# First mixture of experts: token numbers in the rows, results scattered to token order by GpSimd, combination by plain loads, tile loop written out

## The chip, the cores and the metric

The kernel runs on one core of a Trainium2 chip. The metric is the device time of one execution in microseconds (us), given as the median of the executions of a kernel. One execution more is recorded by the hardware profiler; its page and its trace are what is read here. Engines are called PE (TensorE, with PEld for its weight loads), DVE (VectorE), ACT (ScalarE), POOL (GpSimd) and SP (SyncE, which issues DMAs); "SPq", "ACTq" are the queues of their sequencers.

## The reference

Two decoder layers over 4 x 1024 tokens of 256 numbers, fp32: cross attention, then self attention with a mixture of experts, cross attention again, and a second mixture of experts in which each expert chooses its tokens. The change lies in the first mixture:

```python
x = _ln(src + attn, n1_g, n1_b)
xr = x.reshape(-1, d)
logits = xr @ moe_gate_w + moe_gate_b
top_v, top_i = jax.lax.top_k(logits, 2)
wts = jax.nn.softmax(top_v, axis=-1)
chosen = jnp.max(top_i, axis=-1)

def expert(W1, B1, G, Bt, W2, B2, rsc):
    hh = xr @ W1 + B1
    hh = jax.nn.gelu(_ln(hh, G, Bt), approximate=False)
    return (hh @ W2 + B2) * rsc + xr
outs = jax.vmap(expert)(w1, b1, ln_g, ln_b, w2, b2, res_scale)
sel = jnp.take_along_axis(outs.transpose(1, 0, 2), chosen[:, None, None], axis=1)[:, 0]
moe = sel * jnp.sum(wts, axis=-1, keepdims=True)
return _ln(x + moe.reshape(b, s, d), n2_g, n2_b)
```

Each of the 4096 tokens goes through one of eight experts (256 to 512 to 256).

## The kernel before

`self_attention_moe` runs stages one after the other, each a block in which the five engines follow their own instruction lists and meet at semaphores. A block ends when all engines are done, and the next starts after it.

`attention_out` makes the rows `src_sb` (128 partitions x 32 tiles x 256) in eight chunks of four tiles. Beside this, SP fills the DRAM buffer `gathered_in` (4992 rows) with zeros from one tile (L1234), and waits for it at the end of the block. The rows must be zero where no token lands.

`route_tokens` computes for each token its slot in a list sorted by expert, each expert's share rounded up to tiles of 128 rows; there are MT = 39 tiles. GpSimd then scatters `src_sb` to `gathered_in` with one indirect DMA for each of the 32 tiles (L1449), while SP loads the experts' weights, 8 MB.

`expert_tiles` works off the 39 tiles. Each engine runs a body for each tile k, with four buffers (U = 4) and a lead of three tiles (AHEAD = 3). The order in each body is written out by hand:

- SP loads the rows of tile k+3 (L1557), once the bias sum of tile k-1 and the transposes of tile k have freed their buffers.
- PE transposes the rows of tile k+3 (L1580), transposes the normalized hidden rows of tile k (L1601), multiplies tile k-1 by the second weights (L1613) and tile k+3 by the first (L1590).
- ACT stores the result of tile k-2 to `gathered_out` (L1646), copies the transposed rows of tile k+3 (L1630), applies the gelu to tile k (L1640).
- DVE finishes tile k-1 (L1682, into the buffer `xb` that holds rows plus bias), normalizes the hidden rows of tile k+2 (L1675), adds the bias of tile k+3 and takes its moments (L1666 to L1671).
- POOL adds the second bias to the rows of tile k+1 (L1719), which writes `xb` and so waits until the store of tile k-3 has landed (`y_stored`), and then makes the reciprocal deviation of tile k+3 (L1710, L1712), for which it waits for the moments.

The number of the expert is read from SBUF into a register of each engine that uses it. The bodies of tiles 4 to 35 stand in a hardware loop of eight rounds; the first four and the last three are written out.

`combine_experts` goes back to token order in eight chunks of four tiles. POOL gathers the results with 32 indirect DMAs (L1761) by the slots, two chunks ahead, and makes the reciprocal deviation of each chunk (L1769, L1773). DVE multiplies the gathered rows by the token's weight and adds `src_sb` (L1795), takes the moments (L1800, L1803), makes the shift (L1820), then the moments of the next chunk, then for its own chunk the product with the gain (L1809) and the sum into `x_sb` (L1811). ACT normalizes (L1784). There are two buffers `z` and one set of the small vectors.

## Time and profile before

| | |
|---|---|
| median of 3 executions | 2141.88 us (2141.66 to 2144.35) |
| profiled execution, its own time | 2131.64 us |
| its span, first to last instruction | 2130.0 us |
| mean granted clock of TensorE | 0.896 of 2.4 GHz |
| busy: PE, DVE, ACT, POOL | 1744.8, 1278.8, 936.2, 450.0 us |
| routing and scatter | 1266.5 to 1319.5 us |
| expert tile loop | 1319.5 to 1494 us |
| combination | 1495.2 to 1561.7 us |

The windows view gives the busy time of each engine in a stretch, with the number of instructions, then the granted clock of TensorE (PEclk), the busy share of the 16 DMA engines and GB/s. The timeline view gives one row for a run of like instructions: start, duration (of a run, from its first start to its last end), engine, line, operation, tile written<-tiles read, count, and in brackets how long the engine had been idle before and what released it ("issue": nothing that the profile shows). The view of a source line gives durations in ns as least/median/most, and for DMAs the time from the start of their issue to landing. Start times count from the span's start.

### The profile page before, as it was taken

Reading aid. Unit: us, or ns where it says so; the run is one execution under the profiler, and the core shown is the slowest. Engines: PE = TensorE matmul, PEld = TensorE weight load, DVE = VectorE, ACT = ScalarE, POOL = GpSimd, SP = SyncE. Lnnn points to the kernel's source line nnn. Section 1 sums busy time; section 2 is a strip of 40 time slices with the busy share of each in tenths; the row PEclk is TensorE's granted clock in tenths of the full one; section 3 lists DMA queues with packets and bytes.
Section 4 is the critical chain, followed back from the end, with each engine's and each line's share of the span. In section 5 each row is a group of like instructions: output and inputs, shape, how many; then the busy total and the mean of one; then the engine's idle time right before and its main releaser. Section 6 shows DMA issues by size and latency. Waiting matters only on the chain. (4 is left out here: it accounts for less than half of the span.)

```text
span 2130.0 us, 30316 instructions
## 1 busy us (share of the span) xinstructions
PE 1744.8 (82%) x10569; PEld 837.0 (39%) x10570; DVE 1278.8 (60%) x2189; ACT 936.2 (44%) x1708; POOL 450.0 (21%) x467
## 2 busy tenths in 40 slices
PE   5899698399999999999997851999057996259997
PEld 3466454022222222222223640677034663146654
DVE  5344344788999998999951450666684554470221
ACT  3423166077777777777774210444243332102110
POOL 4200044710000000000001435333752001020443
PEclk8899899599999999999999975999579998657999
DMA  4000068712111221112104016121200003310452
GB/s 133 1 1 2 16 210 297 157 23 50 36 37 36 54 54 36 37 36 53 20 1 172 1 49 235 55 64 57 76 10 1 2 2 120 130 31 11 102 135 30
DMA packets 114592, 137.07 MB, mean 64 GB/s; under 512 B 16672, under 2 KB 90656, under 8 KB 114208
## 3 DMA queue, kind: packets, MB, share of 16 engines
q1 hardware_dynamic: 99632, 113.47, 19.3%
q0 software_dynamic: 9216, 16.79, 3.4%
q10 hardware_dynamic: 5616, 5.11, 0.7%
q8 instruction: 80, 1.31, 0.3%
q14 instruction: 48, 0.39, 0.1%
HBM read 78.31 MB, written 56.89 MB: 63 GB/s over the span
## 5 line engine op out<-in xcount | busy, mean ns | idle before, releaser
L984 DVE TENSOR_REDUCE sa_mhalf<-sa_a 128x2 f32<-128x1024 f32 x512 | 602.4, 1221 | 63.9 <-PE sa_a L1093 60.9
L1071 ACT ACTIVATE sa_e<-sa_b 128x512 f32<-128x512 f32 x1024 | 532.0, 602 | 207.2 <-PE sa_b L1120 203.0
L1120 PE MATMUL sa_b<-sa_q,sa_k 112*128 112x512 bf16 x1024 | 310.7, 385 | 3.8 <-ACT sa_e L1071 3.8
L1130 PE MATMUL sa_ops<-sa_e,sa_v 128*17 128x512 f32 x2048 | 270.3, 599 | 6.6 <-ACT sa_e L1071 1.3
L1093 PE MATMUL sa_a<-sa_k,sa_q 48*128 48x512 bf16 x1024 | 176.7, 398 | 44.2 <-DMA sa_k<-k_parts 24.9
L1120 PEld LDWEIGHTS sa_b<-sa_q,sa_k 112*128 112x128 bf16 x1024 | 83.9, 97 | 278.9 <-ACT sa_e L1071 231.6
L1245 POOL TENSOR_TENSOR ao_var<-ao_mv,x_eps_pow 128x4 f32<-128x4 f32 x8 | 1.6, 202 | 762.0 <-DVE ao_mv L1314 762.0
L213 DVE TENSOR_REDUCE xa_mx<-xa_rows 128x16 f32<-128x1024 f32 x64 | 78.3, 1224 | 98.6 <-PE xa_rows L445 98.6
L1093 PEld LDWEIGHTS sa_a<-sa_k,sa_q 48*128 48x128 bf16 x1024 | 43.9, 93 | 193.6 <-DVE sa_mhalf L984 78.8
L360 ACT ACTIVATE xa_pT<-xa_cols 128x1024 f32<-128x1024 f32 x64 | 62.1, 1022 | 84.9 <-PE xa_cols L477 84.9
L2475 DVE TENSOR_TENSOR sw_hT<-sw_p,sw_act 128x512 f32<-128x512 f32 x32 | 22.1, 692 | 102.0 <-PE sw_p L2420 102.0
L1590 PE MATMUL ex_hps<-ew_w,ex_xT 128*128 x156 | 77.3, 619 | 1.9 <-ACT ex_xT L1630 1.9
L445 PE MATMUL xa_rows<-xa_kblk,xa_qT 64*128 64x256 f32 x512 | 73.1, 407 | 6.1 <-DVE xa_mx L213 5.3
L544 PE MATMUL xa_cols<-c_ctxT,c_wts 128*128 128x256 f32 x16 | 7.4, 646 | 85.7 <-PEq L43 72.2
L1613 PE MATMUL ex_yps<-ew_w,ex_hT 128*128 x312 | 73.9, 380 | 1.8 <-ACT ex_hT L1640 1.8
L2388 POOL DMA_INDIRECT out_x<-sw_yo,tc_idx x32 | 49.9, 1558 | 105.7 <-DVE sw_yo L2482 98.7
L2464 ACT ACTIVATE sw_act<-sw_p 128x512 f32<-128x512 f32 x32 | 19.1, 597 | 118.9 <-PE sw_p L2414 118.9
L1630 ACT ACTIVATE ex_xT<-ex_xps 128x256 f32<-128x256 f32 x39 | 15.0, 384 | 126.0 <-PE ex_xps L1580 126.0
L1640 ACT ACTIVATE ex_hT<-ex_tps,sm_bt,sm_g 128x128 f32<-128x128 f32 x156 | 58.8, 457 | 20.9 <-PE ex_tps L1601 17.3
L2414 PE MATMUL sw_p<-sw_xT,tc_w 128*128 128x512 f32 x128 | 62.0, 608 | 1.2 <-ACT sw_xT L2453 1.2
L514 PE MATMUL xa_front<-c_wts,xa_oS 128*128 128x256 f32 x256 | 59.5, 386 | 2.6 <-DVE xa_oS L228 2.6
L1130 PEld LDWEIGHTS sa_ops<-sa_e,sa_v 128*17 128x17 f32 x2048 | 34.9, 95 | 67.2 <-ACT sa_e L1071 54.1
(326 smaller groups left out, 2735.3 us busy)
## 6 DMA issues: line engine op xcount, KB each, us to landing
k_parts<-sp_kpart SPq DMA_DIRECT2D x96, 128.0 KB, 1.8
sa_q<-q_parts SPq DMA_DIRECT2D x64, 192.0 KB, 5.2
sa_k<-k_parts SPq DMA_DIRECT2D x64, 192.0 KB, 5.6
tc_w<-in_L_ffn_W SPq DMA_DIRECT2D x24, 512.0 KB, 6.5
q_parts<-sp_qpart SPq DMA_DIRECT2D x16, 384.0 KB, 3.1
expert_in<-ao_zero SPq DMA_DIRECT2D x1, 4992.0 KB, 23.1
expert_out<-ex_xb ACTq DMA_DIRECT2D x39, 128.0 KB, 1.7
v_groups<-sp_vt SPq DMA_DIRECT2D x8, 544.0 KB, 4.0
```

Of the source, the lines that this page charges most:

```text
L213: nc.vector.tensor_reduce(mx[:, t], rows[:].rearrange("p r (n k) -> p (r n) k", k=SC), axis=X, op=ALU.max).then_inc(max_done, 1)
L360: nc.scalar.activation(pT[:, 4 * half + 2 * part:4 * half + 2 * part + 2], cols[:, 2 * part:2 * part + 2], ACT.Exp, scale=SCALE).then_inc( ...
L445: last = nc.tensor.matmul(rows[:, r, half * D:(half + 1) * D], qT[part, half, tokens], kblk[part, c // 2, half, CT * r:CT * (r + 1)], star ...
L514: last = nc.tensor.matmul(front[:, bank, (t % 2) * D:(t % 2 + 1) * D], oS[:, k, t * P:(t + 1) * P], wts[:, 3, k], start=(k == 0), stop=(k ...
L984: nc.vector.tensor_reduce(mhalf[par][:, half, head:head + PAIRED + 1:PAIRED, t], aps[at][:], axis=X, op=ALU.max).then_inc(a_used, 1)
L1071: nc.scalar.activation(ex[kt % 2][:, head], bps[(2 * (2 * s + qc) + i) % 3][:], ACT.Exp, scale=SCALE).then_inc(exp_done, 1)
L1093: last = nc.tensor.matmul(aps[at][:, h // PAIRED], qs[s][rows, h, q0:q0 + P], ks[s][rows, h, half * CW:(half + 1) * CW], start=True, stop= ...
L1120: nc.tensor.matmul(bps[(2 * (2 * s + qc) + i) % 3][:], ks[s][:, head, kt * P:(kt + 1) * P], qs[s][:, head, qc * CW:(qc + 1) * CW], start=T ...
L1130: last = nc.tensor.matmul(ops[32 * head:32 * head + VW], vs[s][:, kt, head], ex[kt % 2][:, head], start=(kt == 0), stop=(kt == KT - 1))
L1590: last = nc.tensor.matmul(hps[j % 2][:], xT[j % 2][:, half], ew["w1"][:, half, ds(e, 1), :], start=(half == 0), stop=(half == HALVES - 1))
L1613: last = nc.tensor.matmul(yps[j % 2][:, 0:D], hT[j % 2][:, f], ew["w2"][:, f, ds(e, 1), :], start=(f == 0), stop=(f == FK - 1))
L2414: last = nc.tensor.matmul(p1[f % 2][:], w1[e % 3][:, half, f * P:(f + 1) * P], xT[e % 2][:, half], start=(half == 0), stop=(half == HALVES ...
```

## The change

The rows of `src_sb`, `gathered_in` and the loaded tiles become 264 numbers long. The eight columns behind the 256 hold the token's number as an integer; rows in which no token lands hold numbers past the last token, from 4096 on, each another one. These are written to DRAM by a second DMA behind the zeros. In the tile loop POOL copies the column of token numbers to a small tile of its own, adds the bias, makes the deviation, and issues the store of tile k-2 itself, as an indirect DMA that scatters the 128 result rows to `moe_out` by token number. ACT stores nothing. Four buffers for the loaded rows are allocated; two of them were spent tiles before. The hardware loop becomes 39 bodies in a row. The combination loads the results with eight plain DMAs on SP's queue, has four buffers `z` and two sets of the small vectors; the product with the gain moves from DVE to POOL, and DVE's last sum for a chunk stands behind the moments of the chunk three later.

```diff
+ROW = D + 8
...
-        zero = sb("zero", [P, D])
+        zero, spare = sb("zero", [P, D]), sb("spare", [P, MT, ROW - D], i32)
...
+                rows = gathered_in.rearrange("(k p) d -> p k d", p=P)
                 sp.wait_ge(zero_made, 1)
-                sp.dma_start(gathered_in.rearrange("(k p) d -> p k d", p=P),
-                             bc(zero[:], 1, [P, MT, D])).then_inc(cleared, 16)
-                sp.wait_ge(cleared, 16)
+                sp.dma_start(rows[:, :, 0:D], bc(zero[:], 1, [P, MT, D])).then_inc(cleared, 16)
+                sp.wait_ge(spare_made, 1)
+                sp.dma_start(rows[:, :, D:ROW], spare[:].bitcast(fp32)).then_inc(cleared, 16)
+                sp.wait_ge(cleared, 32)
...
+                nc.gpsimd.iota(spare[:], [[P, MT], [0, ROW - D]], base=TOKENS, channel_multiplier=1).then_inc(spare_made, 1)
...
+                nc.gpsimd.iota(src_rows[:, :, D:ROW].bitcast(i32), [[P, TILES], [0, ROW - D]], base=0, channel_multiplier=1
+                               ).then_inc(iota_made, 1)
+                pool.wait_ge(iota_made, 3)
                 pool.wait_ge(slots_ready, 1)
                 for t in range(TILES):
                     pool.indirect_dma_start(out=gathered_in, out_offset=bass.IndirectOffsetOnAxis(ap=slot_i[:, t:t + 1], axis=0),
-                                            in_=src_sb[:, t, :], in_offset=None).then_inc(scattered, 16)
+                                            in_=src_rows[:, t, :], in_offset=None).then_inc(scattered, 16)
...
-        xg = [b[:].rearrange("p t e -> p (t e)") for b in spent] + [sb(f"xg{i}", [P, D]) for i in range(len(spent), U)]
+        xg = [sb(f"xg{i}", [P, ROW]) for i in range(U)]
+        token = [sb(f"token{i}", [P, 1], i32) for i in range(U)]
...
-            for j in range(U):
-                body(j, 0, j, True)
-            with eng.Fori(1, MT // U) as i:
-                for j in range(U):
-                    body(i * U + j, i, j, True)
-            for k in range(MT // U * U, MT):
-                body(k, k // U, k % U, False)
+            for k in range(MT):
+                body(k, k // U, k % U, k + AHEAD < MT)
...
-                def store(k, j):
-                    act.wait_ge(y_ready, k + 3)
-                    act.dma_start(gathered_out[ds(P * k, P), :], xb[j][:]).then_inc(y_stored[j], 16)
-
                 def body(k, turn, j, ahead):
-                    if later(k, 2):
-                        store(k - 2, (j - 2) % U)
...
                 def add_b2(k, turn, j):
                     e = expert(pool, k)
                     pool.wait_ge(x_loaded[j], 16 * (turn + 1))
-                    if later(k, U):
+                    if k >= U:
                         pool.wait_ge(y_stored[j], 16 * turn)
-                    nc.gpsimd.tensor_tensor(xb[j][:], xg[j][:], ew["b2"][:, ds(e, 1), :].rearrange("p o f -> p (o f)"),
+                    nc.gpsimd.tensor_copy(token[j][:], xg[j][:, D:D + 1].bitcast(i32)).then_inc(token_kept, 1)
+                    pool.wait_ge(token_kept, k + 1)
+                    nc.gpsimd.tensor_tensor(xb[j][:], xg[j][:, 0:D], ew["b2"][:, ds(e, 1), :].rearrange("p o f -> p (o f)"),
                                             ALU.add).then_inc(xb_ready, 1)
 
                 def body(k, turn, j, ahead):
-                    if not isinstance(k, int) or k + 1 < MT:
+                    if k + 1 < MT:
                         add_b2(k + 1, turn + (j + 1) // U, (j + 1) % U)
                     if ahead:
                         make_rstd(k + AHEAD, (j + AHEAD) % U)
+                    if k >= 2:
+                        scatter(k - 2, (j - 2) % U)
+
+                def scatter(k, j):
+
+                    pool.wait_ge(y_ready, k + 3)
+                    pool.indirect_dma_start(out=moe_out, out_offset=bass.IndirectOffsetOnAxis(ap=token[j][:, 0:1], axis=0),
+                                            in_=xb[j][:], in_offset=None).then_inc(y_stored[j], 16)
 
                 pool.wait_ge(ew["b2_scaled"], 1)
                 pool.wait_ge(y_ready, 2)
                 for k in range(AHEAD):
                     make_rstd(k, k)
                 turns(pool, body)
-
-
-def combine_experts(nc, x_sb, src_sb, eps_pow, w, wsum, slot_i, gathered_out):
-
+                for k in range(MT - 2, MT):
+                    scatter(k, k % U)
...
-                sp.dma_start(n2g[:], w["n2_g"].partition_broadcast(P)).then_inc(loaded, 16)
+                for c in range(CHUNKS):
+                    sp.dma_start(yg[:, CT * c:CT * (c + 1)], moe_out[CW * c:CW * (c + 1)].rearrange("(t p) d -> p t d", p=P)
+                                 ).then_inc(y_loaded[c], 16)
+                    if c == 1:
+                        sp.dma_start(n2g[:], w["n2_g"].partition_broadcast(P)).then_inc(loaded, 16)
...
-                def gather(c):
-                    for t in range(CT * c, CT * (c + 1)):
-                        pool.indirect_dma_start(out=yg[:, t, :], out_offset=None, in_=gathered_out,
-                                                in_offset=bass.IndirectOffsetOnAxis(ap=slot_i[:, t:t + 1], axis=0)
-                                                ).then_inc(gathered[c], 16)
-
-                gather(0)
-                gather(1)
+                def invert(c):
+                    par = c % 2
+                    pool.wait_ge(ln_stats, CT * (c + 1))
+                    nc.gpsimd.tensor_tensor(var[par][:], mv[par][:, :, 1], eps_pow[:, 0], ALU.add).then_inc(var_done, 1)
+                    pool.wait_ge(var_done, c + 1)
+                    if c >= 2:
+                        pool.wait_ge(zn_ready, CT * (c - 1))
+                    nc.gpsimd.tensor_tensor(rstd[par][:], var[par][:], eps_pow[:, 1], ALU.pow).then_inc(rstd_ready, 1)
+
+                def scale(c):
+                    zs = z[c % BUFFERS]
+                    pool.wait_ge(zn_ready, CT * (c + 1))
+                    nc.gpsimd.tensor_tensor(zs[:], zs[:], bc(n2g[:], 1, [P, CT, D]), ALU.mult).then_inc(zg_ready, 1)
+
+                invert(0)
+                pool.wait_ge(loaded, 16)
                 for c in range(CHUNKS):
-                    pool.wait_ge(ln_stats, CT * (c + 1))
-                    nc.gpsimd.tensor_tensor(var[:], mv[:, :, 1], eps_pow[:, 0], ALU.add).then_inc(var_done, 1)
-                    pool.wait_ge(var_done, c + 1)
-                    if c >= 1:
-                        pool.wait_ge(zn_ready, CT * c)
-                    nc.gpsimd.tensor_tensor(rstd[:], var[:], eps_pow[:, 1], ALU.pow).then_inc(rstd_ready, 1)
-                    if c + 2 < CHUNKS:
-                        gather(c + 2)
+                    if c + 1 < CHUNKS:
+                        invert(c + 1)
+                    scale(c)
...
-                    dve.wait_ge(gathered[c], 16 * CT)
-                    if c >= 2:
-                        dve.wait_ge(x_done, c - 1)
+                    dve.wait_ge(y_loaded[c], 16)
...
+                def make_shift(c):
+                    par = c % 2
                     dve.wait_ge(rstd_ready, c + 1)
                     dve.wait_ge(ln_stats, CT * (c + 1))
+                    if c >= 2:
+                        dve.wait_ge(zn_ready, CT * (c - 1))
+                    nc.vector.scalar_tensor_tensor(out=shift[par][:], in0=mv[par][:, :, 0], scalar=-1.0, in1=rstd[par][:],
+                                                   op0=ALU.mult, op1=ALU.mult).then_inc(shift_ready, 1)
+                    dve.wait_ge(shift_ready, c + 1)
+
+                def finish(c):
+
+                    xs = x_sb[:, CT * c:CT * (c + 1), :]
+                    dve.wait_ge(zg_ready, c + 1)
+                    nc.vector.tensor_tensor(xs, xs, z[c % BUFFERS][:], ALU.add).then_inc(x_done, 1)
+                    dve.wait_ge(x_done, c + 1)
+
+                moments(0)
+                moments(1)
+                for c in range(CHUNKS):
+                    make_shift(c)
+                    if c + 2 < CHUNKS:
+                        moments(c + 2)
                     if c >= 1:
-                        dve.wait_ge(zn_ready, CT * c)
-                    nc.vector.scalar_tensor_tensor(out=shift[:], in0=mv[:, :, 0], scalar=-1.0, in1=rstd[:], op0=ALU.mult,
-                                                   op1=ALU.mult).then_inc(shift_ready, 1)
-                    if c + 1 < CHUNKS:
-                        dve.wait_ge(shift_ready, c + 1)
-                        moments(c + 1)
-                    finish(c)
+                        finish(c - 1)
+                finish(CHUNKS - 1)
...
-    gathered_in = nc.dram_tensor("expert_in", (MT * P, D), fp32, kind="Internal").ap()
-    gathered_out = nc.dram_tensor("expert_out", (MT * P, D), fp32, kind="Internal").ap()
+    gathered_in = nc.dram_tensor("expert_in", (MT * P, ROW), fp32, kind="Internal").ap()
+    moe_out = nc.dram_tensor("moe_out", (TOKENS + MT * P, D), fp32, kind="Internal").ap()
```

## Rows read from the trace of the kernel before

**Rows 1.** Windows: the tile loop, and a later stretch with TensorE partly idle.

```profile
1340.00:1475.00 135.00, 135.00 (x594) 94.94 (x593) 93.74 (x166) 61.33 (x163) 50.28 (x99) 1.00 0.21 65
...
1600.00:1620.00 20.00, 13.62 (x48) 6.74 (x48) 10.02 (x6) 6.43 (x9) 10.81 (x5) 1.00 0.00 0
```

**Rows 2.** Timeline of PE in the tile loop.

```profile
1469.81 1.89 PE L1613 MATMUL ex_yps<-ew_w,ex_hT 128*128 x8
...
1473.91 1.89 PE L1613 MATMUL ex_yps<-ew_w,ex_hT 128*128 x8
```

**Rows 3.** Timeline of POOL in the tile loop.

```profile
1389.46 0.19 POOL L1710 TENSOR_TENSOR ex_var<-ex_mv,x_eps_pow 128x1 f32<-128x1 f32 x1 [2.03 <-DVE ex_mv L1671]
1389.73 0.55 POOL L1712 TENSOR_TENSOR ex_rstd<-ex_var,x_eps_pow 128x1 f32<-128x1 f32 x1
1390.55 0.73 POOL L1719 TENSOR_TENSOR ex_xb<-ex_xg,sm_b 128x256 f32<-128x256 f32 x1 [0.27 <-issue]
```

**Rows 4.** Line L1449, the routing's scatters: the last six, then all 32.

```profile
L1449 POOL DMA_INDIRECT expert_in<-sm_src,sm_slot_i x6: 956/960/960, 1307.3 to 1313.7; - x6
...
DMA to landing us min/median/max: 2.4/2.4/2.4
...
DMA to landing us min/median/max: 2.4/5.5/6.6
```

**Rows 5.** Landing of the gathers (L1761), and of the last stage's accumulating scatters (DMA view).

```profile
DMA to landing us min/median/max: 2.7/2.8/3.4
...
out_x<-sw_yo,tc_idx POOLq DMA_INDIRECT x32, 3.9
```

**Rows 6.** Timeline of all engines in a middle chunk of the combination.

```profile
1522.14 1.02 POOL L1761 DMA_INDIRECT co_yg<-expert_out,sm_slot_i  x1 [0.19 <-issue]
...
1522.18 1.67 DVE L1795 SCALAR_TENSOR_TENSOR co_z<-co_yg,sm_wsum,sm_src 128x256 f32<-128x256 f32 x4
...
1525.36 1.20 DVE L1809 TENSOR_TENSOR co_z<-co_z,co_n2g 128x1024 f32<-128x1024 f32 x1
...
1529.22 1.67 DVE L1795 SCALAR_TENSOR_TENSOR co_z<-co_yg,sm_wsum,sm_src 128x256 f32<-128x256 f32 x4
```

**Rows 7.** The same timeline: a power by itself, then the last chunk.

```profile
1520.91 1.03 POOL L1773 TENSOR_TENSOR co_rstd<-co_var,x_eps_pow 128x4 f32<-128x4 f32 x1
...
1554.80 1.22 DVE L1811 TENSOR_TENSOR x_x<-x_x,co_z 128x1024 f32<-128x1024 f32 x1
1554.90 1.99 POOL L1773 TENSOR_TENSOR co_rstd<-co_var,x_eps_pow 128x4 f32<-128x4 f32 x1
...
1557.13 2.07 ACT L1784 ACTIVATE co_z<-co_z,co_shift,co_rstd 128x256 f32<-128x256 f32 x4 [4.71 <-DVE co_shift L1820]
...
1560.49 1.22 DVE L1811 TENSOR_TENSOR x_x<-x_x,co_z 128x1024 f32<-128x1024 f32 x1
```

**Rows 8.** The same timeline: the combination's start.

```profile
1495.24 0.34 SPq L1755 DMA_DIRECT2D co_n2g<-in_L_ffn_n_g  x1
...
1502.74 1.67 DVE L1795 SCALAR_TENSOR_TENSOR co_z<-co_yg,sm_wsum,sm_src 128x256 f32<-128x256 f32 x4 [10.80 <-DMA co_yg<-expert_out,sm_slot_i]
```

**Rows 9.** A plain load of 512 KB (DMA view), and a POOL product of 128x1024 (line L1252).

```profile
x_x<-in_x SPq DMA_DIRECT2D x1, 512.0 KB, 3.9
...
L1252 POOL TENSOR_TENSOR ao_xr<-ao_xr,ao_n1g x8: 2337/2342/2349, 1165.2 to 1253.2; 128x1024 f32<-128x1024 f32 x8
```

**Rows 10.** Timeline of the tile loop's end, and ACT's stores in the DMA view.

```profile
1483.88 0.55 POOL L1712 TENSOR_TENSOR ex_rstd<-ex_var,x_eps_pow 128x1 f32<-128x1 f32 x1
...
1490.23 2.09 ACTq L1646 DMA_DIRECT2D expert_out<-ex_xb  x2
...
expert_out<-ex_xb ACTq DMA_DIRECT2D x39, 128.0 KB, 1.7
```

**Rows 11.** DMA view: the zeros. Timeline: the routing's first scatter.

```profile
expert_in<-ao_zero SPq DMA_DIRECT2D x1, 4992.0 KB, 23.1
...
1274.18 1.24 POOL L1449 DMA_INDIRECT expert_in<-sm_src,sm_slot_i  x1 [7.25 <-DVE sm_slot_i L1501]
```

More of the change, by code:

```diff
@@ L1658, in _ @@
                 turns(act, body)
-                for k in range(MT - 2, MT):
-                    store(k, k % U)
             @block.vector
@@ L1734, in _, with combine_experts @@
                 turns(pool, body)
-def combine_experts(nc, x_sb, src_sb, eps_pow, w, wsum, slot_i, gathered_out):
+                for k in range(MT - 2, MT):
+                    scatter(k, k % U)
+def combine_experts(nc, x_sb, src_sb, eps_pow, w, wsum, moe_out):
+    BUFFERS = 4
     with ExitStack() as ctx:
@@ L1743, in combine_experts @@
         yg = sb("yg", [P, TILES, D])
-        z = [sb(f"z{i}", [P, CT, D]) for i in range(2)]
-        stats, mv = sb("stats", [P, CT, 6]), sb("mv", [P, CT, 2])
-        var, rstd, shift = sb("var", [P, CT]), sb("rstd", [P, CT]), sb("shift", [P, CT])
+        z = [sb(f"z{i}", [P, CT, D]) for i in range(BUFFERS)]
+        stats, mv = ([sb(f"{n}{i}", [P, CT, k]) for i in range(2)] for n, k in (("stats", 6), ("mv", 2)))
+        var, rstd, shift = ([sb(f"{n}{i}", [P, CT]) for i in range(2)] for n in ("var", "rstd", "shift"))
         loaded, z_ready, stats_done, ln_stats = sem("loaded"), sem("z_ready"), sem("stats_done"), sem("ln_stats")
-        gathered = [sem(f"gathered{c}") for c in range(CHUNKS)]
-        var_done, rstd_ready, zn_ready, zg_ready, x_done = (sem("var_done"), sem("rstd_ready"), sem("zn_ready"),
-                                                                      sem("zg_ready"), sem("x_done"))
-        shift_ready = sem("shift_ready")
+        y_loaded = [sem(f"y_loaded{c}") for c in range(CHUNKS)]
+        var_done, rstd_ready, shift_ready = sem("var_done"), sem("rstd_ready"), sem("shift_ready")
+        zn_ready, zg_ready, x_done = sem("zn_ready"), sem("zg_ready"), sem("x_done")
         with nc.Block() as block:
@@ L1779, in _ @@
                 for c in range(CHUNKS):
+                    zs, par = z[c % BUFFERS], c % 2
                     act.wait_ge(shift_ready, c + 1)
@@ L1783, in _ @@
                     for t in range(CT):
-                        nc.scalar.activation(z[c % 2][:, t], z[c % 2][:, t], ACT.Identity, bias=shift[:, t:t + 1],
-                                             scale=rstd[:, t:t + 1]).then_inc(zn_ready, 1)
+                        nc.scalar.activation(zs[:, t], zs[:, t], ACT.Identity, bias=shift[par][:, t:t + 1],
+                                             scale=rstd[par][:, t:t + 1]).then_inc(zn_ready, 1)
             @block.vector
@@ L1789, in moments @@
                 def moments(c):
-                    dve.wait_ge(gathered[c], 16 * CT)
-                    if c >= 2:
-                        dve.wait_ge(x_done, c - 1)
+                    zs, par = z[c % BUFFERS], c % 2
+                    dve.wait_ge(y_loaded[c], 16)
                     for t in range(CT):
-                        nc.vector.scalar_tensor_tensor(out=z[c % 2][:, t], in0=yg[:, CT * c + t],
+                        nc.vector.scalar_tensor_tensor(out=zs[:, t], in0=yg[:, CT * c + t],
                                                        scalar=wsum[:, CT * c + t:CT * c + t + 1], in1=src_sb[:, CT * c + t],
@@ L1897, in self_attention_moe @@
         own = Kit(nc, ctx, "sm_")
-        src_sb = own.sb("src", [P, TILES, D])
+        src_rows = own.sb("src", [P, TILES, ROW])
+        src_sb = src_rows[:, :, 0:D]
         self_projections(nc, x_sb, src_sb, ident, eps_pow, w, q_parts, k_parts, v_dram)
```

46 lines of the change are left out of this document (23 added, 23 removed).

## The prediction

> **What bounds the kernel now.** I read four views in this order. The windows by stage show that the first mixture of experts runs in two parts with different limits. In the expert tile loop TensorE is busy for all 135 of 135 us at a granted clock of 1.00 (2.4 GHz), while GpSimd works 50 us [rows 1]. The timeline of TensorE shows one tile every 1473.91 - 1469.81 = 4.10 us, back to back, so the register instructions that the loop adds to its queue are covered [rows 2]. The timeline of GpSimd shows for each tile a variance of 0.19 us, a power of 0.55 us and the bias sum of 0.73 us, with 2.03 us idle before the variance because VectorE is late [rows 3]. The timeline of the combination shows the other limit: VectorE's chunks start 1529.22 - 1522.18 = 7.04 us apart [rows 6], and the stage lasts from 1495.24 [rows 8] to 1560.49 + 1.22 = 1561.71 us [rows 7], 66.5 us.
>
> **What is added to GpSimd's queue, and who waits.** In each tile's body GpSimd now issues the bias sum for tile k+1, the reciprocal deviation for tile k+3 and last the scatter of tile k-2. The next body begins with the bias sum for tile k+2, which needs the buffer that tile k-2 leaves free: four buffers, so it is the scatter issued just before. Until now ScalarE issued that store early in its body and nobody stood behind it. Now GpSimd stands still while its own scatter lands, and behind it in the queue is the reciprocal deviation of tile k+4, on which VectorE's normalization and then TensorE's transpose hang. This makes a cycle that lies on one engine:
>
> gap before the scatter 0.19 [rows 6] + landing L + wake-up 0.05 (an estimate, between the zero and the 0.19 of that gap) + token copy with its own wait 0.27 (the variance, as narrow, starts 0.27 before the power that waits for it: 1389.73 - 1389.46) + bias sum 0.73 + gap 0.07 (the same 0.27 less the 0.19 of the variance, rounded) + variance 0.27 + power 0.55 [rows 3] = 2.13 + L.
>
> For L the trace has scatters of the same 128 rows of 1 KB. The last six of the routing, with the weight loads over, land 2.4 us after their start, all six [rows 4]; beside those loads the median of all is 5.5 [rows 4]. Gathers beside VectorE's work land in 2.7 to 3.4, and accumulating scatters at a median of 3.9 [rows 5]. In the tile loop the DMA engines are 21% busy [rows 1], so the nearest row is 2.4. To it I add 0.07, since a transfer behind a compute instruction takes 1.02 [rows 6] against 0.96 [rows 4], and 0.13 for VectorE's normalization, which starts just then; this last is an estimate between nothing and the 0.6 by which a gather's landing varies [rows 5]. L = 2.6, with ends of 2.4 and 3.4. The cycle is 4.73 us (4.53 to 5.53), 0.63 over the 4.10 of now (0.43 to 1.43). It starts with the deviation of tile 5 and runs to that of tile 38, 33 times: 33 x 0.63 = **+20.8 us** (14.2 to 47.2).
>
> The row of the routing says 2.4 to 2.6 for such a transfer. The Trainium skill (DMA: Bandwidth & Descriptors, section Anatomy of one DMA) gives 2.0 us plus the bytes over 436 GB/s for a transfer that GpSimd issues, most of it the wait for the write to be confirmed: 2.3 us for 128 KB. By that alone the cycle would be an estimated 4.43 and the loop's term 10.9.
>
> **The loop's end.** After the last deviation GpSimd still has two bias sums, each behind a landing, and four more scatters. With L = 2.6: 0.19 + 2.6 + 0.05 + 0.27 + 0.73 = 3.84, then 3.75 with a gap of 0.10, then after 0.1 three scatters spaced 1.26 (0.96 [rows 4] and a gap of 0.30) and the last one's 2.4: 13.9 us. Now it is from 1484.43 (1483.88 + 0.55) to the last store, issued about 1492.0 within the row of two issues, + 1.7 = 1493.7 [rows 10], 9.3 us. That is **+4.6** (4.4 to 6.2). TensorE's own last tiles fit inside.
>
> **The combination.** Removed: 32 gathers on GpSimd, 1.26 us apart, and the z*gain product on VectorE. Added: eight plain loads of 512 KB on SP, and the product on GpSimd at 2.34 us for this shape [rows 9]. The first load lands 3.9 us after its issue [rows 9], against the 7.5 us from SP's first issue to VectorE's first instruction [rows 8]; the other seven are covered, since one chunk of data moves while VectorE needs over 4 us for one. VectorE's moments take 1525.36 - 1522.18 = 3.2 us, its last sum 1.22 [rows 7] and a short gap, 1.23, the shift about 0.2.
>
> If nothing collides, VectorE sets the pace: 3.9 + 2 x 3.2 + 3.4 (shift and moments) + 5 x 4.65 (with the last sum) + 8.3 for the last two chunks (two shifts, two sums, ScalarE's 2.07 [rows 7] and GpSimd's 2.34 in line, and gaps) = 45.3, a gain of 21.2. But the last chunk shows a collision: beside VectorE's sum of two SBUF operands, which runs from 1554.80 to 1556.02, the power that takes 1.03 us elsewhere takes 1.99, and ends 0.87 after that sum [rows 7]. So they take turns. What then takes turns in one chunk: first product 1.6, variance 0.25, power 1.03, GpSimd's product 2.34, last sum 1.23 = 6.45 us. Sum: 3.9 + 6.4 + 3.4 + 5 x 6.45 + 9.6 (for the last two chunks power 1.03 and variance 0.25, two products, three sums of 1.23) = 55.6, a gain of **10.9**. I take this one, since the row shows it. The least is the 3 us of the earlier start.
>
> The row, power 1.99 for 1.03, is what the Trainium skill (SBUF — State Buffer, section SBUF: two separate sides) states as a rule: a VectorE instruction with two SBUF inputs and a GpSimd one that reads SBUF share a port pair, and the one that starts first holds it to its end. The trace agrees here. By the same rule the product on GpSimd, more than twice as long as the power, is a holder too, which speaks against this edit.
>
> **What costs nothing.** The spare columns: 4992 pieces of 32 bytes; the zeros, 4992 pieces of 1 KB, are issued right before them at 1147 us and land in 23.1 us [rows 11]. As many short pieces may take as long; if each took three times as long, both would be in by 1147 + 23 + 70 = 1240, and the block ends at 1265. Rows of 1056 bytes instead of 1024 are 3% more in the routing, where GpSimd's issue sets the time. The token numbers are written in the 7.25 us that GpSimd idles before the slots are ready [rows 11]. The first spare numbers come before the wait for the vectors. The loop written out takes register instructions from queues that are covered; below nothing it can't cost, and above, if code came late, it would stand as gaps on TensorE. ScalarE's 39 stores go; ScalarE waits for TensorE anyway.
>
> **Sum.** +20.8 + 4.6 - 10.9 = +14.5 us against this execution's 2131.64 (its span is 2130.0). The median of the runs is 2141.88, 10.2 above; the sum is put on that: **2156.4**.
>
> **The rivals.**
> (1) Faster: the landing is covered. The place is the wait for the stored buffer ahead of the bias sum; it decides nothing as long as 2.13 + L is below 4.10, that is L under 1.97. For it: ScalarE's plain store lands in 1.7 [rows 10]. Against: no indirect transfer of the trace is under 2.4. Then the loop stays at 4.10, its end costs 0.7, and the combination gives 10.9: 2131.7; with the free combination 2121.4.
> (2) Much slower: in the loop the scatter lands as beside other traffic, in 3.9 [rows 5] or 5.5 [rows 4]. The cycle is 6.03 or 7.63, the loop +63.7 or +116.5; with 7 to 10 for the end, about 2203 or 2258. Against: those rows have other DMA traffic or an accumulation.
> (3) TensorE's clock falls in the new gaps of 0.6 us. At 1.2 GHz a tile would need 8.2 us: 33 x 4.1 - 10.9 + 5 = +129, 2271. Against: over 20 us with TensorE busy for only 13.62 the clock stays at 1.00 [rows 1].
>
> **Chances.** Forecast 0.71, its own range 14.2 + 4.4 - 21.2 = -2.6 to 47.2 + 6.2 - 3 = +50.4, so 2139 to 2192; (1) 0.18; (2) 0.08; (3) 0.03. A measurement of this kernel tells about 0.2%, 4.3 us, from no change. Of the forecast's 0.71 I put 0.12 within that bound (short landing and free combination) and 0.02 below. Faster 0.18 + 0.02 = 0.20, same 0.12, slower 0.68. The range begins at 2132, which leaves out about half of the first rival, and ends at 2192, which leaves out (2) and (3): 0.09 + 0.08 + 0.03 = 0.20.
>
> **What would show it.** Right: in the tile loop GpSimd is idle before the token copy, released by the scatter's landing; the tiles are 4.5 to 5.5 us apart; TensorE waits about 0.6 us before the transposes of the normalized rows, and VectorE's normalization waits for the deviation; the scatters land in 2.4 to 3.4. In the combination VectorE's last sum waits for GpSimd's product and chunks are about 6.4 apart. Wrong: tiles still 4.10 apart with the copy released at once (rival 1), landings near 4 or more (2), a clock under 0.9 in the loop (3), or chunks at 4.7.

## The result and the profile after

The changed kernel takes 2161.4 us in the median of 4 executions (2156.96 to 2166.82), the kernel before beside it 2142.48: ratio 1.0088, 95% interval 1.0064 to 1.0113, 18.9 us slower. The forecast was 2156.4, with 0.68 on slower. The slowdown is under 1% and some four times the 0.2% that such a measurement can tell.

The two profiled executions, 2131.64 and 2166.82 us, are 35 us apart, more than the medians. A second trace of the kernel before (the last experiment, its own time 2146.93) shows why: unchanged stages ran longer in it too. Against that second trace every stage can be set beside its own. The marks are VectorE's `rt_mark` in the routing, SP's first load of rows in the tile loop, the start of GpSimd's power in the deviations of tiles 5 and 38, SP's first issue in the combination and the end of VectorE's last sum there:

| stage (us) | before, second trace | after | difference |
|---|---|---|---|
| up to the routing's first mark | 1271.1 | 1271.3 | +0.2 |
| to the tile loop's first load | 52.6 | 53.2 | +0.7 |
| to the power of tile 5 | 28.9 | 27.3 | -1.6 |
| 33 tiles, to the power of tile 38 | 135.9 | 160.1 | +24.2 |
| to the combination's first issue | 11.4 | 18.4 | +7.0 |
| combination | 66.8 | 53.2 | -13.5 |
| all behind it | 578.6 | 581.5 | +2.9 |
| span | 2145.2 | 2165.1 | +19.9 |

The five rows that the change touches make up +16.8 us; the +2.9 behind the combination lies in stages of unchanged code. The timeline of POOL in the tile loop after the change, which answers to [rows 3]:

```profile
1391.54 1.05 POOL L1732 DMA_INDIRECT moe_out<-ex_xb,ex_token  x1 [0.19 <-issue]
1394.17 0.18 POOL L1716 COPY ex_token<-ex_xg 128x1 int32<-128x1 int32 x1 [1.58 <-DMA moe_out<-ex_xb,ex_token]
1394.54 0.72 POOL L1718 TENSOR_TENSOR ex_xb<-ex_xg,sm_b 128x256 f32<-128x256 f32 x1 [0.19 <-POOL ex_token L1716]
1395.22 0.18 POOL L1707 TENSOR_TENSOR ex_var<-ex_mv,x_eps_pow 128x1 f32<-128x1 f32 x1
1395.49 0.57 POOL L1709 TENSOR_TENSOR ex_rstd<-ex_var,x_eps_pow 128x1 f32<-128x1 f32 x1
1396.25 1.06 POOL L1732 DMA_INDIRECT moe_out<-ex_xb,ex_token  x1 [0.19 <-issue]
...
1512.69 1.30 POOL L1732 DMA_INDIRECT moe_out<-ex_xb,ex_token  x1 [0.19 <-issue]
...
1524.68 0.97 POOL L1732 DMA_INDIRECT moe_out<-ex_xb,ex_token  x1 [0.30 <-issue]
```

The cycle stands there in full. The only long idle time is the 1.58 us before the token copy, released by the landing of the scatter just issued; everything else follows with gaps of 0.2. From scatter to scatter it is 1396.25 - 1391.54 = 4.71 us. The variance, which before had waited 2 us for VectorE, now starts with no wait in 31 of the 33 turns. The waits from 1352 to 1512 us (engine, line, releaser: us in total, times, longest) and the windows view of the loop:

```profile
POOL ex_token L1716 <- DMA moe_out<-ex_xb,ex_token: 53.5, 33, 2.2
...
PEld ex_xps L1585 <- DMA ex_xg<-expert_in: 26.8, 30, 1.8
```

```profile
1345.00:1510.00 165.00, 152.91 (x624) 98.88 (x624) 87.81 (x175) 65.52 (x174) 92.05 (x169) 1.00 0.18 55
```

33 waits for the landing, one a tile. TensorE is no longer busy throughout (152.9 of 165 us against 135 of 135 in [rows 1]), and the longest waits of its weight loads (PEld) are for the load of its next rows. The granted clock stays at 1.00, 2.4 GHz.

A middle chunk of the combination, timeline of all engines, which answers to [rows 6]:

```profile
1551.01 0.16 DVE L1830 SCALAR_TENSOR_TENSOR co_shift<-co_mv,co_rstd 128x4 f32<-128x4 f32 x1
1551.11 1.01 POOL L1780 TENSOR_TENSOR co_rstd<-co_var,x_eps_pow 128x4 f32<-128x4 f32 x1
1551.21 1.67 DVE L1812 SCALAR_TENSOR_TENSOR co_z<-co_yg,sm_wsum,sm_src 128x256 f32<-128x256 f32 x4
1551.21 2.08 ACT L1802 ACTIVATE co_z<-co_z,co_shift,co_rstd 128x256 f32<-128x256 f32 x4 [3.73 <-DVE co_shift L1830]
1552.79 1.40 DVE L1817 BATCH_NORM_STATS2 co_stats<-co_z 128x6 f32<-128x256 f32 x4
1553.36 2.34 POOL L1785 TENSOR_TENSOR co_z<-co_z,co_n2g 128x1024 f32<-128x1024 f32 x1 [1.24 <-ACT co_z L1802]
...
1554.39 2.39 DVE L1838 TENSOR_TENSOR x_x<-x_x,co_z 128x1024 f32<-128x1024 f32 x1
...
1556.81 0.17 DVE L1830 SCALAR_TENSOR_TENSOR co_shift<-co_mv,co_rstd 128x4 f32<-128x4 f32 x1
```

A chunk takes 1556.81 - 1551.01 = 5.80 us, before 7.04. VectorE's last sum, 1.22 us by itself [rows 7], shows 2.39: it starts inside GpSimd's product and ends 1.08 us behind the product's end (1555.70). So the wait for the other engine stands in the sum's duration and not in an idle time.

### The profile page after: what moved, and what is told of

Read it like the earlier page. It is cut to its first block and busy times, and to the rows that moved or that the text cites. A ratio compares the mean times of both kernels' runs of the same rounds, so it can differ in the third digit from the quotient of the medians.

```text
span 2165.1 us, 29730 instructions
## 1 busy us (share of the span) xinstructions
PE 1761.1 (81%) x10569; PEld 839.6 (39%) x10569; DVE 1269.8 (59%) x2180; ACT 936.3 (43%) x1707; POOL 483.5 (22%) x522
## 5 line engine op out<-in xcount | busy, mean ns | idle before, releaser
L1585 PE MATMUL ex_xps<-x_ident,ex_xg 128*128 128x128 f32 x78 | 16.6, 295 | 59.7 <-DMA ex_xg<-expert_in 59.4
L1618 PEld LDWEIGHTS ex_yps<-ew_w,ex_hT 128*128 128x128 f32 x312 | 56.2, 190 | 20.7 <-issue 14.5
L421 PE MATMUL xa_rows<-xa_xnT,c_wts 128*128 128x512 f32 x128 | 63.4, 645 | 0.0
## 6 DMA issues: line engine op xcount, KB each, us to landing
expert_in<-ao_zero SPq DMA_DIRECT2D x1, 4992.0 KB, 26.1
```

The costliest lines, as they stand in the source:

```text
L1618: last = nc.tensor.matmul(yps[j % 2][:, 0:D], hT[j % 2][:, f], ew["w2"][:, f, ds(e, 1), :], start=(f == 0), stop=(f == FK - 1))
```

## The experiments

The first four ran on one chip, the next four on a second, the last two on a third. The kernel before took 2141.2, 2132.4 and 2141.2 us there, so ratios are compared and not times.

**The changed kernel again** (no edit).

> The changed kernel once more, with nothing edited, as the control of the others and to see how much its executions differ. Expected: 2161 us (2157 to 2167) against 2142, ratio 1.009, and a span whose tile loop takes 160 us from the 5th to the 38th power of the loop, as before. The stage that chooses the second mixture's tokens took 49.4 us in one profiled execution and 60.6 in the other though no line of it changed: if that is a stall that some executions have, it will be near one of these two values here, whatever the time of the first mixture.

Measured: 2161.4 us, ratio 1.0095 (1.0073 to 1.0116). The 33 tiles took 159.4 us, the combination 53.3, the choice of tokens 60.5. The slowdown and its stages repeat.

**The new combination alone, on the kernel before.**

The body of `combine_experts` is the changed kernel's; the rows that it loads are in slot order, so tokens get other tokens' rows.

```diff
...
-        combine_experts(nc, x_sb, src_sb, eps_pow, w, wsum, slot_i, gathered_out)
+        combine_experts(nc, x_sb, src_sb, eps_pow, w, wsum, gathered_out)
```

> The kernel before, with only the combination of the changed kernel: it loads 512 KB blocks of four tiles in row order and gathers nothing. It leaves out the return to token order, so that every token gets another token's row; the amount of work is the same. Theory: the gain of the combination is its own, 66.5 us become 53.2 as in the changed kernel, and the time is 13 us under the kernel before, 2129 us (ratio 0.994). Rival: part of the 13 us hangs on what comes ahead of the stage in the changed kernel (scatters in place of stores), so that the stage takes 55 us or more here and the ratio is 0.995 or above.

Measured: ratio 0.9948 (0.9932 to 0.9964), 11.9 us less in the medians; in the trace the stage takes 1548.16 - 1494.85 = 53.3 us. The gain is the stage's own, whatever comes ahead of it.

**The scatter one turn earlier.**

```diff
-                    if k >= 2:
-                        scatter(k - 2, (j - 2) % U)
+                    if k >= 1:
+                        scatter(k - 1, (j - 1) % U)
...
-                for k in range(MT - 2, MT):
-                    scatter(k, k % U)
+                scatter(MT - 1, (MT - 1) % U)
```

> The changed kernel, with each tile's scatter issued one turn earlier on GpSimd (tile k-1's at the end of turn k, not tile k-2's). Theory (the tile loop is a cycle on GpSimd, of some 3.1 us of work and 1.6 us of waiting for the landing of the scatter that has just been issued): the landing now has a turn's time, the 1.6 us go, the tiles come 4.1 us apart as in the kernel before, bound by TensorE, and the time is 33 x 0.74 = 24 to 27 us under the changed kernel, near 2135 us and below the kernel before. Rival A (the longer period comes from GpSimd's added work, the 1056-byte rows or the loop written out): the tiles stay 4.7 to 4.9 us apart and the time near 2161. Rival B (the earlier scatter makes GpSimd wait for VectorE's sum of a tile just done): the wait for the landing is replaced by one for the sum, tiles 4.3 to 4.6 apart, time 2144 to 2155.

Measured: 2132.1 us, ratio 0.9953 (0.9936 to 0.9971): 29 us under the changed kernel on the same chip, and faster than the kernel before. The 33 tiles take 138.3 us. From the waits of 1352 to 1482 us:

```profile
POOL ex_var L1707 <- DVE ex_mv L1668: 31.1, 31, 2.0
```

GpSimd's long wait is again the one for VectorE, as before the change. 27 of the 33 periods are 4.09 to 4.13 us, one is 3.75 and five are 4.45 to 5.39.

**Rings of five for results and token numbers.**

```diff
-        token = [sb(f"token{i}", [P, 1], i32) for i in range(U)]
-        xb = [sb(f"xb{i}", [P, D]) for i in range(U)]
+        token = [sb(f"token{i}", [P, 1], i32) for i in range(5)]
+        xb = [sb(f"xb{i}", [P, D]) for i in range(5)]
...
-                    if k >= U:
-                        pool.wait_ge(y_stored[j], 16 * turn)
+                    if k >= 5:
+                        pool.wait_ge(y_stored[(k - 5) % U], 16 * ((k - 5) // U + 1))
...
```

> The changed kernel, with rings of five result tiles and five token tiles in place of four, so that the token copy of tile k waits for the landing of the scatter of tile k-5 and not k-4; the order of every engine's work stays. Theory (the landing of the scatter sets the period): the copy no longer waits, the tiles come 4.1 us apart (GpSimd's own work is 3.1 us of it), and the time is 24 to 27 us under the changed kernel, near 2135 us. Rival (work and not the wait sets the period): tiles 4.7 to 4.9 us apart, time near 2161.

Measured: 2132.6 us, ratio 0.9964 (0.9952 to 0.9977). The timeline of POOL in the loop and, from the waits of 1352 to 1482 us, what POOL waits for:

```profile
1402.27 1.04 POOL L1732 DMA_INDIRECT moe_out<-ex_xb,ex_token  x1 [0.19 <-issue]
1403.32 0.20 POOL L1716 COPY ex_token<-ex_xg 128x1 int32<-128x1 int32 x1
1403.71 0.72 POOL L1718 TENSOR_TENSOR ex_xb<-ex_xg,sm_b 128x256 f32<-128x256 f32 x1 [0.19 <-POOL ex_token L1716]
1405.35 0.19 POOL L1707 TENSOR_TENSOR ex_var<-ex_mv,x_eps_pow 128x1 f32<-128x1 f32 x1 [0.92 <-DVE ex_mv L1668]
1405.62 0.57 POOL L1709 TENSOR_TENSOR ex_rstd<-ex_var,x_eps_pow 128x1 f32<-128x1 f32 x1
1406.38 1.05 POOL L1732 DMA_INDIRECT moe_out<-ex_xb,ex_token  x1 [0.20 <-issue]
```

```profile
POOL ex_var L1707 <- DVE ex_mv L1668: 29.7, 31, 1.6
```

The same six instructions with the same durations, and the copy follows the scatter at once. The period is 1406.38 - 1402.27 = 4.11; the slack is back where it was before, ahead of the variance. Two different edits, one in the order and one in the buffers, remove the same wait and give the same time: the wait, and not GpSimd's added work, was the cost. The 33 tiles take 136.9 us. With either edit 1.0 to 2.4 us are left over the 135.9 of before: PEld still waits 5.7 us (here) and 7.1 us (the scatter one turn earlier) in all for the load of its rows, each in 19 waits. The bias sum, behind which that load stands, starts 2.2 us after the power here (0.76 to the scatter, then 1403.71 - 1402.27), and 0.8 in [rows 3]; that this is why the loads come late was not tried.

**The tile loop alone written out** (on the kernel before).

```diff
-            with eng.Fori(1, MT // U) as i:
-                for j in range(U):
-                    body(i * U + j, i, j, True)
...
+            for k in range(MT):
+                body(k, k // U, k % U, k + AHEAD < MT)
```

> The kernel before, with only the tile loop written out: all 40 turns stand in the program, with constants for the tile's number. Theory (writing the loop out is free): 2141 us, ratio 1.000 within 0.001, 33 tiles in 135.5 us. Rival A (the registers and waits on registers cost something in the loop): a ratio of 0.998 or below. Rival B (ten times the code has to be fetched and holds an engine back): 1.002 or above, with gaps of no releaser ahead of the loop's instructions. It is also a second trace of the stages that no experiment touches: the choice of tokens took 49.4 us in the profiled execution before, and 57 to 61 us in the five traces since.

Measured: ratio 0.9994 (0.9982 to 1.0006), 33 tiles in 135.3 us (the loop has 39 turns, not the 40 of the expectation). Writing it out is free here.

**ScalarE's plain stores in place of the scatters.**

```diff
+                def store(k, j):
+                    act.wait_ge(y_ready, k + 3)
+                    act.dma_start(moe_out[ds(P * k, P), :], xb[j][:]).then_inc(y_stored[j], 16)
...
+                    if k >= 2:
+                        store(k - 2, (j - 2) % U)
...
-                    if k >= 2:
-                        scatter(k - 2, (j - 2) % U)
...
```

> The changed kernel, with GpSimd's scatter of each tile replaced by ScalarE's plain store of it to rows in slot order, two turns behind as in the kernel before; rows of 1056 bytes, the copy of the token numbers and the written-out loop stay. It leaves out the return to token order. Theory (the scatters alone cost the time): 33 tiles in 135.5 us as before, and 10.8 us, not 17.8, from the loop's last normalization factor to the combination's first load, since the block no longer ends on GpSimd's transfers; with the combination's 13 us gained the time is 2129 us, as of the kernel before with the new combination alone. Rival (wide rows, token copy or bias sum behind it cost something themselves): 2133 us or more, with a period of 4.2 us or above. For the handover at the loop's end: if the 2 us more that it takes hang on the engine whose transfers end the block, they go here; if on the rows or on the combination's plain loads, they stay.

Measured: ratio 0.9932 (0.9916 to 0.9948). 33 tiles in 135.3 us and 1494.93 - 1483.41 = 11.5 us from the last power's start to the combination (11.4 in the table's trace of before). The wide rows and the token copy cost nothing, and PEld's waits for its rows are down to 0.2 us. The loop's end, timelines of DVE and of SP's queue here, and below them POOL's last scatter and SP in the version with rings of five:

```profile
1491.01 0.48 DVE L1687 SCALAR_TENSOR_TENSOR ex_xb<-ex_yps,sm_rs,ex_xb 128x256 f32<-128x256 f32 x1 [1.45 <-PE ex_yps L1618]
...
1494.93 0.93 SPq L1764 DMA_DIRECT2D co_yg<-moe_out  x2
```

```profile
1490.30 0.48 DVE L1679 SCALAR_TENSOR_TENSOR ex_xb<-ex_yps,sm_rs,ex_xb 128x256 f32<-128x256 f32 x1 [1.57 <-PE ex_yps L1618]
...
1493.06 0.97 POOL L1732 DMA_INDIRECT moe_out<-ex_xb,ex_token  x1 [0.31 <-issue]
...
1498.70 0.93 SPq L1766 DMA_DIRECT2D co_yg<-moe_out  x2
```

From the start of VectorE's last sum to the next block's first issue it takes 3.9 us with ScalarE's store and 8.4 with GpSimd's scatters. Of these, 2.76 us go by until the last scatter starts, and 5.64 from there on, of which the landing is 2.4. The new combination behind the old stores also starts 11.4 us after the last power's start, so its plain loads are not what delays it.

**The combination's product on VectorE** (with the rings of five).

```diff
-                    nc.gpsimd.tensor_tensor(zs[:], zs[:], bc(n2g[:], 1, [P, CT, D]), ALU.mult).then_inc(zg_ready, 1)
...
+                    nc.vector.tensor_tensor(zs[:], zs[:], bc(n2g[:], 1, [P, CT, D]), ALU.mult).then_inc(zg_ready, 1)
+                    dve.wait_ge(zg_ready, c + 1)
```

> The changed kernel with rings of five, in which the combination's product with the gain row is moved from GpSimd to VectorE, ahead of the last sum; GpSimd keeps the addition of epsilon and the power. In the trace the product of a chunk (2.34 us) and the last sum of the chunk before (2.39 us) overlap by 1.3 us, and the sum then needs 1.1 us more. Theory (these two work in turns, one being held while the other runs): on VectorE alone both take 1.1 us each, the chunk stays at 3.4 + 2.2 = 5.6 us against 5.8, and the time is within 2 us of the version with rings of five (2133 us), against before a ratio of 0.995 to 0.997. Rival (GpSimd's product runs beside VectorE for free and slows it little): the chunk becomes 5.8 + 1.1 to 2.3 = 6.9 us or more, and the time 9 us longer or more, 2142 us.

Measured: ratio 0.9946 (0.9927 to 0.9964), just under the expected 0.995 to 0.997; the stage takes 50.8 us against 53.2. Timeline of a middle chunk:

```profile
1526.99 0.16 DVE L1821 SCALAR_TENSOR_TENSOR co_shift<-co_mv,co_rstd 128x4 f32<-128x4 f32 x1
1527.18 1.67 DVE L1803 SCALAR_TENSOR_TENSOR co_z<-co_yg,sm_wsum,sm_src 128x256 f32<-128x256 f32 x4
...
1530.37 1.19 DVE L1830 TENSOR_TENSOR co_z<-co_z,co_n2g 128x1024 f32<-128x1024 f32 x1
1531.59 1.23 DVE L1832 TENSOR_TENSOR x_x<-x_x,co_z 128x1024 f32<-128x1024 f32 x1
1531.69 1.99 POOL L1780 TENSOR_TENSOR co_rstd<-co_var,x_eps_pow 128x4 f32<-128x4 f32 x1
1532.85 0.16 DVE L1821 SCALAR_TENSOR_TENSOR co_shift<-co_mv,co_rstd 128x4 f32<-128x4 f32 x1
```

Product and sum on one engine take 1.19 + 1.23 us, as much as the held sum alone took; the chunk stays at 5.86. GpSimd's help with the product bought nothing in the steady part, and the stage is 2.4 us shorter through its end: from the last shift on it takes 5.2 us in place of 7.9.

**The last sum first** (with the rings of five, product on GpSimd).

```diff
+                    if c >= 1:
+                        finish(c - 1)
                     if c + 2 < CHUNKS:
                         moments(c + 2)
-                    if c >= 1:
-                        finish(c - 1)
```

> The changed kernel with rings of five, in which VectorE does the last sum of a chunk right behind the shift of the next, ahead of the four multiply-adds and statistics and not behind them. Theory (the last sum is held by GpSimd's product that runs at the same time): now GpSimd has finished the product of the chunk before and waits for ScalarE, so that the sum takes 1.1 us in place of 2.4, the chunk 4.5 to 4.9 us in place of 5.8, and the time is 6 to 9 us less than with rings of five alone, near 2125 us. Rival (the sum's 2.4 us are its own length, or GpSimd's chain of power, wait for ScalarE and product sets the chunk): the chunk stays at 5.5 us or more and the time within 3 us of 2133.

Measured: ratio 0.9965 (0.9952 to 0.9979), that of the rings of five alone (0.9964), and in the trace the stage takes 56.1 us, 2.9 longer. The expected gain of 6 to 9 us did not come. The time of 2124.3 us lies near the expected 2125 only because the kernel before takes 9 us less on this chip. The rival's sign, a chunk of 5.5 us or more, came true, and neither of its two reasons. Timeline of two chunks:

```profile
1525.04 1.23 DVE L1838 TENSOR_TENSOR x_x<-x_x,co_z 128x1024 f32<-128x1024 f32 x1
...
1526.30 1.67 DVE L1812 SCALAR_TENSOR_TENSOR co_z<-co_yg,sm_wsum,sm_src 128x256 f32<-128x256 f32 x4
...
1527.62 2.55 POOL L1785 TENSOR_TENSOR co_z<-co_z,co_n2g 128x1024 f32<-128x1024 f32 x1
1527.89 1.40 DVE L1817 BATCH_NORM_STATS2 co_stats<-co_z 128x6 f32<-128x256 f32 x4
...
1529.48 0.71 DVE L1830 SCALAR_TENSOR_TENSOR co_shift<-co_mv,co_rstd 128x4 f32<-128x4 f32 x1
...
1530.28 1.23 DVE L1838 TENSOR_TENSOR x_x<-x_x,co_z 128x1024 f32<-128x1024 f32 x1
...
1531.54 3.76 DVE L1812 SCALAR_TENSOR_TENSOR co_z<-co_yg,sm_wsum,sm_src 128x256 f32<-128x256 f32 x4
1532.38 2.63 POOL L1785 TENSOR_TENSOR co_z<-co_z,co_n2g 128x1024 f32<-128x1024 f32 x1
```

The hold is shown, and the gain is not there. The sum does take 1.23 us. But now the product falls on the next instructions with two inputs in SBUF: in one chunk it holds the shift, 0.71 for 0.16, in the next the multiply-adds, 3.76 for 1.67. The statistics, with one input, run beside it at their 1.40. From sum to sum the chunks alternate between 5.24 and 6.69 us. The product is paid by whichever of these instructions it meets.

**Three edits together**: rings of five, the earlier scatter, the product on VectorE.

> The changed kernel with three edits at once: rings of five, each scatter one turn earlier on GpSimd, and the combination's product on VectorE. Theory (scatters off the cycle, and the last of them nearer to the last tile's sum): with rings of five alone the last scatter began 2.3 us after the last sum, with the earlier scatter 1.5 us after its start; the loop's end comes 1.0 to 1.3 us earlier than with two of the edits, ratio to before 0.993 to 0.995. Rival (the earlier scatter makes GpSimd wait for VectorE's sum now and then): no gain over two of the edits, ratio 0.9946 or above.

Measured: 2132.0 us, ratio 0.9949 (0.9935 to 0.9962). The trace has the gain expected: the last scatter starts 1.5 us after the last sum's start (1494.32 - 1492.83) and not 2.8, and the loop's end takes 13.6 us in place of 14.9. In the ratio 1.3 us can't be told, and the rival's 0.9946 or above is met as well; so this version and the one with two of the edits stand level. By the ratios both are some 11 us under the kernel before, and 30 under the changed one.

**The kernel before again** (no edit).

> The kernel before, unedited, for a second trace of it. In the first four experiments, which shared a chip, the stage that chooses the second mixture's tokens took 57 to 61 us and the kernel before 2141; in the next four, on another chip, the stage took 49 us and the kernel before 2132. Theory (this stage depends on the chip and not on the change): its length here goes with the time of the kernel before, near 59 us if that is 2141 and near 49 if it is 2132. Rival (the length is tied to the kernel's version): 49 us with a time of 2141, or 59 with 2132. Ratio 1.000 within 0.001.

Measured: ratio 1.0003, with the kernel before at 2141.2 us, and the choice of tokens takes 58.6 us. Its waits of TensorE between 1890 and 1945 us:

```profile
PE ct_slots L2201 <- DVE ct_ids L2330: 7.0, 1, 7.0
PE ct_slots L2201 <- issue: 5.3, 9, 1.2
...
PE ct_spread L2215 <- issue: 1.9, 4, 0.6
```

The waits with no releaser are absent in the second chip's traces that were read for it (the loop written out, the product on VectorE). The stage took 49.4 us in the first profiled execution of before and 60.6 in that of after. So of the 35 us between them, about 11 belong to this stage and to no line of the change.

## Why the prediction was right

The direction, the places and the main mechanism were right. Each of the three terms was smaller than what was measured, and the errors partly cancel: +3.4 us in the loop and +2.4 at its end against -2.6 in the combination. That the time came within 5 us of the forecast is in part luck.

**The cycle in the tile loop** was forecast at 2.13 + 2.6 = 4.73 us. Where nothing disturbs it, it is 4.70: 20 of 33 periods lie between 4.68 and 4.73. From the scatter's start to the copy it takes 2.63 us, forecast 2.65; the copy to the bias sum 0.37, not 0.27; the bias sum to the variance 0.68, not 0.80. That landing and not work is what is waited for was shown by the two edits that take the wait away. The Trainium skill (DMA: Bandwidth & Descriptors, section Anatomy of one DMA) would have had an estimated 2.3 us for the landing. The trace has 2.4 at least, 2.5 in the median and 3.2 at most, and the row of the routing was the better guide.

**The loop's term** of +20.8 us measured +24.2. The step that failed is the one that took the same landing for all 33 turns: 13 periods are 4.95 to 5.51 us. In seven the scatter itself shows 1.30 us in place of 1.05, in four it lands 0.3 to 0.65 us later; that makes 3.4 us. In the other two the variance waits 0.5 and 0.7 us for VectorE's moments, and in one of the seven the bias sum starts 0.33 us late, 1.6 us that no landing explains. Together it is 160.1 - 33 x 4.70 = 5.0 us. Two expected signs were wrong too. VectorE's normalization, which was to wait for the deviation, does so in 4 turns, 1.4 us in all. TensorE, which was to wait 0.6 us for the normalized rows, waits for the rows that SP loads, since SP's load stands behind the bias sum. The cycle on GpSimd is the one forecast; the path from it to TensorE is another.

**The loop's end**, +4.6, measured +7.0. It counted to the landing of the last transfer and took for granted that the next block follows alike. The last scatter starts 12.2 us after the last power's end, forecast 11.5: 0.7 us. The rest, 1.7, is the handover: from the last landing to the next block's first issue it is 1495.24 - 1493.7 = 1.5 us behind ScalarE's stores [rows 8, 10] and 1530.33 - (1524.68 + 2.4) = 3.2 behind GpSimd's scatters. It was to be had from the trace of before: the routing ends on such scatters, its last starting at 1313.7 [rows 4], and the tile loop begins at 1319.5 in that trace, 5.9 us later, against 5.65 here.

**The combination**, -10.9, measured -13.5 (-13.2 against the first trace). The choice of the turn-taking model over the free one was right: the free one would have had chunks of 4.65 us, the stage 45.3. What failed is the list of what takes turns. The power was counted in as taking turns, but from the third shift on it runs at its 1.01 us beside the four multiply-adds at their 1.67. Even the last sum, the instruction that held the power in [rows 7], runs beside it at its own length where the power has started first, in the last chunks here:

```profile
1574.34 1.01 POOL L1780 TENSOR_TENSOR co_rstd<-co_var,x_eps_pow 128x4 f32<-128x4 f32 x1
1574.43 1.22 DVE L1838 TENSOR_TENSOR x_x<-x_x,co_z 128x1024 f32<-128x1024 f32 x1
```

What is held is the last sum, by the product: shift 0.2, ScalarE 2.08, product 2.34, and the sum's remaining 1.08, with gaps 5.8 against the 6.45 forecast.

The Trainium skill (SBUF — State Buffer, section SBUF: two separate sides) speaks of an exclusive port for a VectorE instruction with two SBUF inputs beside a GpSimd one; by it either the power or the multiply-adds would have been held. The trace agrees for sum, shift and multiply-adds beside the product, and for a power that starts behind the sum (1.99 us). It does not for a power that has started first: neither the multiply-adds nor the sum are held by it. The forecast said that the rule speaks against this edit, and the product moved back to VectorE gains 2.4 us.

**What was costed at nothing** held: the loop written out (0.9994), wide rows and token copy (135.3 us for 33 tiles with them), the spare columns (the zeros land in 26.1 us and the numbers behind them in 29.2, both hidden). The routing's part is +0.7. Not foreseen was a gain of 1.6 us at the loop's start (last section).

**The rivals.** The covered landing, the first rival, is what the earlier scatter and the rings of five make: its condition, landing under the slack, was not met with four buffers and an issue in the turn just ahead, and is met with one turn more. The scatter's landing never came near 3.9, and the clock stayed.

## What to carry to other kernels

When a store is moved to another engine, look up who waits for its landing and what stands behind that wait on the same engine: an engine that waits for the transfer it has just issued pays the landing in full on every turn. Here one turn of distance, by order or by one more buffer, took the period from 4.70 us back to 4.11. The change lost 31 us in this way and at the block's end, and gained 13 with the other half; an edit with two halves is worth taking apart, since the half that gains also gains alone. And before an elementwise step goes to GpSimd to relieve VectorE, look at which VectorE instructions with two SBUF operands it will run beside, and add its time to theirs: here the relief was nothing.

## What the runs showed of the hardware that was not expected

- A block whose last transfers come from GpSimd hands over 1.7 us later than one that ends on ScalarE's stores. From the start of the last scatter to the next block's first issue it was 5.64 or 5.65 us in seven traces. What GpSimd does in that time no view shows.
- A scatter's own duration in the loop is 1.05 us or 1.30. In both traces of the changed kernel it is 1.30 where VectorE's normalization (0.54 us) started 0.13 to 0.16 us ahead of it, and 1.05 where it was 0.12 or less; with 0.05 us ahead, in the version with the product on VectorE (1477.58 and 1477.63), it is 1.05. Beside the bias sum the same normalization took 0.97 us in the median before.
- The choice of the second mixture's tokens, with the same code, took 56.9 to 60.5 us in the traces of two of the chips and 49.2 to 49.3 in four traces of the third; where it was looked for, TensorE has gaps that no releaser explains on the former and none on the latter. What differs between the chips isn't settled. A difference of 10 us between two single profiled executions means nothing until each stage is compared.
- TensorE starts the loop at a granted clock of 0.50, 1.2 GHz. Before, the first products of the second tile still took 3.77 us; after the change, with the same instructions ahead of them, they took 1.98. Timelines of TensorE of the second trace of before, and of after:

```profile
1327.06 3.77 PE L1590 MATMUL ex_hps<-ew_w,ex_xT 128*128 x4 [0.56 <-ACT ex_xT L1630]
1330.63 0.63 PE L1580 MATMUL ex_xps<-x_ident,sm_top 128*128 128x128 f32 x2
1331.83 3.78 PE L1590 MATMUL ex_hps<-ew_w,ex_xT 128*128 x4 [0.56 <-ACT ex_xT L1630]
```

```profile
1328.00 3.78 PE L1595 MATMUL ex_hps<-ew_w,ex_xT 128*128 x4 [0.56 <-ACT ex_xT L1635]
1331.57 0.63 PE L1585 MATMUL ex_xps<-x_ident,ex_xg 128*128 128x128 f32 x2
1332.76 1.98 PE L1595 MATMUL ex_hps<-ew_w,ex_xT 128*128 x4 [0.56 <-ACT ex_xT L1635]
```

  The windows view has a granted clock of 0.51 from 1331.8 to 1335.6 us before, and 1.00 from 1332.7 to 1334.7 after. The clock rose one tile earlier, worth 1.8 us, and that is the gain at the loop's start. It was so with plain stores as well, and not with the loop alone written out; the cause was not tried.
